# Two feed-forward stages around a state-space layer: layer 1 multiplied once per batch for z and for its twist

## The reference

```python
gf = _global_net(z.mean(axis=1), ...)                 # one number for a batch
out = z
for _ in range(3):                                    # NUM_CYCLES
    h = gelu(out @ w1 + b1); h = gelu(h @ w2 + b2); h = gelu(h @ w3 + b3)
    tf = sigmoid(h @ w4 + b4)                         # one number for a token
    coupling = 0.1 + adaptive_range * (0.7 * gf + 0.3 * tf - 0.5) * 2.0
    out = out + coupling * twist(out)                 # [o_r,o_i,p_r,p_i] -> [p_r,-p_i,-o_r,o_i]
```

## Time and profile before

| | |
|---|---|
| median of 3 runs | 1359.43 us (1358.84 to 1360.23) |
| the profiled execution | 1361.13 us, its span from first to last instruction 1359.1 us |
| TensorE matmul busy | 1133.3 us, 83% of the span |
| VectorE busy | 1149.4 us, 85% |
| ScalarE busy | 737.0 us, 54% |
| GpSimd busy | 871.9 us, 64% |
| mean granted TensorE clock | 0.949 of full speed |

### The profile page before, as it was taken

The page is one execution under the profiler, slowest core; times in us unless marked ns, Lnnn a source line. Parts: engine busy times, 40 slices in busy tenths (PEclk is TensorE's granted clock), DMA queues, the critical chain, the costliest instruction groups (busy, mean ns, idle before and its releaser), DMA issues. The chain is left out here.

```text
span 1359.1 us, 10889 instructions
## 1 busy us (share of the span) xinstructions
PE 1133.3 (83%) x2880; PEld 491.7 (36%) x2880; DVE 1149.4 (85%) x1628; ACT 737.0 (54%) x1267; POOL 871.9 (64%) x390
## 2 busy tenths in 40 slices
PE   3999985769778889878978987987896978799997
PEld 2344432223333334324324333433432423434443
DVE  4656676399999999999999999999999999746556
ACT  2554444757655756755656674665674433355442
POOL 0000000699989999998999999899999998000000
PEclk9999996798999999999999989999998988999998
DMA  6000000444535444354453544435435442000001
GB/s 201 0 1 1 0 0 1 140 135 146 180 102 185 132 149 155 124 185 134 146 179 113 174 146 139 151 124 186 154 127 184 155 156 78 0 0 0 32 31 62
DMA packets 46940, 146.47 MB, mean 108 GB/s; under 512 B 4448, under 2 KB 13280, under 8 KB 46880
## 3 DMA queue, kind: packets, MB, share of 16 engines
q1 hardware_dynamic: 46384, 144.96, 31.8%
q10 hardware_dynamic: 496, 0.82, 0.2%
HBM read 141.05 MB, written 4.72 MB: 107 GB/s over the span
## 5 line engine op out<-in xcount | busy, mean ns | idle before, releaser
L905 POOL TENSOR_TENSOR m_u<-m_dx,m_brow 128x1024 f32<-128x1024 f32 x256 | 596.7, 2355 | 1.0 <-DVE m_a_bank L988 0.9
L791 ACT ACTIVATE m_a_bank<-m_delta,m_negA 128x512 f32<-128x512 f32 x512 | 335.0, 683 | 171.6 <-DVE m_hc L1000 131.3
L1134 PE MATMUL m_y_bank<-m_hc,ident 128*128 128x512 f32 x640 | 333.1, 646 | 103.7 <-DVE m_hc L1000 103.7
L917 POOL TENSOR_TENSOR m_hc_pool<-m_hid,m_crow 128x1024 f32<-128x1024 f32 x96 | 226.0, 2354 | 28.5 <-DVE m_hid L988 28.1
L1134 PEld LDWEIGHTS m_y_bank<-m_hc,ident 128*128 128x128 f32 x640 | 120.1, 201 | 290.7 <-DVE m_hc L1000 170.5
L1000 DVE TENSOR_TENSOR m_hc<-m_a_bank,m_crow 128x512 f32<-128x512 f32 x320 | 202.5, 673 | 0.0
L926 POOL TENSOR_TENSOR m_dx<-m_delta,m_x 128x1024 f32<-128x1024 f32 x16 | 37.7, 2357 | 249.5 <-ACT m_delta L863 249.5
L988 DVE TENSOR_TENSOR_SCAN m_a_bank<-m_a_bank,m_carry,m_u 128x512 f32<-128x512 f32 x160 | 196.1, 1270 | 1.1 <-ACT m_a_bank L791 0.8
L988 DVE TENSOR_TENSOR_SCAN m_a_bank<-m_a_bank,m_u 128x512 f32<-128x512 f32 x160 | 186.6, 1212 | 7.1 <-POOL m_u L905 3.5
L1134 PE MATMUL m_y_bank<-m_hc_pool,ident 128*128 128x512 f32 x384 | 184.4, 603 | 5.6 <-POOL m_hc_pool L917 5.6
L333 PE MATMUL f_bank<-f_state,w 128*128 128x512 f32 x384 | 181.9, 603 | 0.0
(11 more groups left out here) (111 smaller groups left out, 1168.8 us busy)
## 6 DMA issues: line engine op xcount, KB each, us to landing
m_brow<-bc_rows SPq DMA_DIRECT2D x128, 512.0 KB, 4.8
m_crow<-bc_rows SPq DMA_DIRECT2D x128, 512.0 KB, 3.9
x_tok<-x_in SPq DMA_DIRECT2D x4, 1024.0 KB, 8.6
out<-x_tok SPq DMA_DIRECT2D x3, 1024.0 KB, 4.4
w<-w_in SPq DMA_DIRECT2D x1, 1024.0 KB, 11.4
out<-x_tok SPq DMA_DIRECT2D x2, 512.0 KB, 3.0
w<-w_in SPq DMA_DIRECT2D x1, 750.0 KB, 10.4
w<-w_in ACTq DMA_DIRECT2D x1, 512.0 KB, 5.9
```

The source lines that it names most:

```text
L791: nc.scalar.activation(a_bank[K % 2][:, j, :], delta[:, i % 2, c, :], ACT.Exp, scale=negA[:, c, n:n + 1]).then_inc(S["a"], 1)
L905: nc.gpsimd.tensor_tensor(u[:, K % U_RING, :, :], dx[:, i % 2, 2 * q:2 * q + 2, :], brow[:, K // 2 % ROW_RING, K % 2, :].unsqueeze(1).to_b ...
L917: nc.gpsimd.tensor_tensor(hc_pool[:, before % POOL_RING, :, :], hid[:, before % POOL_RING, :, :], crow[:, K // 2 % ROW_RING, K % 2, :].uns ...
L1134: op = nc.tensor.matmul(y_bank[:, j, :], ident[:, :], source[:, before % ring, j, :], start=False, stop=K % PASS == PASS - 1)
```

## The change

Only `ffn` changes, and the order of the channels in the inputs: the host permutes the quarters of the channels so that `twist` of the two channel halves `[z0, z1]` is `[z1, -z0]`.

- TensorE multiplies `A = z @ w1` and `B = twist(z) @ w1` once for each batch and half (kinds `A` and `B`, L440 and L441, four multiplications each, `B` with a negated copy `neg_w` of half the weights). ScalarE copies both from PSUM into SBUF (`a` and `b_`, 1024 elements in one instruction, L570). `layer1` is gone from the steps.
- `gelu1` (L508) reads SBUF: `a` in cycle 0, `a1` in cycle 1, `a` again in cycle 2.
- VectorE makes these. `update` (L242, L255, L257) runs in cycles 0 and 1 only: the coupling, written over the tanh, then one product and one sum of 1024 elements, with the coupling row repeated for both output halves. After cycle 0, `turn` (L265, L270) brings `b_` to the next state's twist with four instructions of 1024.
- `z_tok` holds all 32 tiles. The last state isn't formed with channels on partitions. SyncE copies one row of each coupling of cycles 0 and 1 into `stack` by DMA, the last tanh goes there too, TensorE transposes `stack` (kind `C`, L448), VectorE works out the coefficients of each token (`coefficients`, 15 instructions of 8 elements), and `finish` applies them in token order: ScalarE `x * scale + bias` (L548, 8 instructions of 256), then VectorE two sums of 128 channels for each tile (L322, L324). For batch 2 (`ALONE`) VectorE does ScalarE's part too (L314).
- The table is now `BESIDE`: (step and place on TensorE, kind, batch, half or layer, step and place on ScalarE). The output is stored in four whole batches.

The core of the diff:

```diff
+    BESIDE = [
...
+        (5, 0, "g", 3, 0, 5, 1), (5, 1, "g", 3, 1, 5, 2), (5, 1, "B", 3, 0, 5, 2), (5, 2, "g", 3, 2, 5, 3),
+        (6, 0, "C", 0, 0, None, None), (6, 1, "B", 3, 1, 6, 2), (7, 0, "C", 1, 0, None, None),
...
+            def normalise(b):
+                for t in range(BT):
+                    o = b * BT + t
+                    nc.vector.tensor_scalar(z_tok[:, o, :], x_tok[:, o, :], moments[:, o, 0:1], rstd[:, o:o + 1],
+                                            ALU.subtract, ALU.mult).then_inc(z_ready, 1)
...
+                b, n = batch(s), coupled(s, h)
+                c = cpl[:, b % 2, half(h)]
+                dve.wait_ge(th_ready, s * HALVES + h + 1)
+                nc.vector.tensor_scalar(c, c, slope[:, 0:1], base[:, b:b + 1], ALU.mult, ALU.add).then_inc(coupling, 1)
+                dve.wait_ge(coupling, n)
...
+                nc.vector.tensor_tensor(to, b_[:, b % AB_RING, :, half(h)], over_m(c), ALU.mult).then_inc(scaled, 1)
+                dve.wait_ge(scaled, n)
+                nc.vector.tensor_tensor(to, to, other, ALU.add).then_inc(a_ready, 1)
+            def turn(s):
...
+                for h in range(HALVES):
+                    nc.vector.tensor_tensor(part[:, h], a[:, b % AB_RING, :, half(h)],
+                                            over_m(cpl[:, b % 2, half(h)]), ALU.mult).then_inc(part_ready, 1)
+                for h in range(HALVES):
+                    from_b = b_[:, b % AB_RING, :, half(h)]
+                    dve.wait_ge(part_ready, turned(s, h))
+                    nc.vector.tensor_tensor(from_b, from_b, part[:, h], ALU.subtract).then_inc(b_ready, 1)
...
+            def coefficients(b):
...
+                dve.wait_ge(beside_done, done_count(("C", b, 0)))
+                if b > 0:
+                    wait_added(dve, b - 1)
...
+                for j in range(2):
+                    nc.vector.tensor_copy(at(j), src[:, :, 32 + j])
+                nc.vector.tensor_scalar(at(2), src[:, :, 0], slope[:, 0:1], base[:, b:b + 1],
+                                        ALU.mult, ALU.add).then_inc(coef_read, 1)
+                dve.wait_ge(coef_read, b + 1)
...
+            def finish(b):
+                coefficients(b)
+                if b == ALONE:
+                    for t in range(BT):
+                        at = b * BT + t
+                        op = nc.vector.scalar_tensor_tensor(x_tok[:, at, :], z_tok[:, at, :], coef[:, 7, t:t + 1],
+                                                            x_tok[:, at, :], ALU.mult, ALU.add)
+                    op.then_inc(first_added, 1)
+                    dve.wait_ge(first_added, 1)
+                for t in range(BT):
+                    at, c = b * BT + t, slice(t, t + 1)
+                    if b != ALONE:
+                        dve.wait_ge(first_act, (b - (b > ALONE)) * BT + t + 1)
+                    nc.vector.scalar_tensor_tensor(x_tok[:, at, :P], z_tok[:, at, P:], coef[:, 8, c], x_tok[:, at, :P],
+                                                   ALU.mult, ALU.add).then_inc(added, 1)
+                    nc.vector.scalar_tensor_tensor(x_tok[:, at, P:], z_tok[:, at, :P], coef[:, 9, c], x_tok[:, at, P:],
+                                                   ALU.mult, ALU.add).then_inc(added, 1)
...
+            for s in range(1, STEPS + 1):
+                if cycle(s - 1) < CYCLES - 1:
                     for h in range(HALVES):
                         update(s - 1, h)
                 if s == 1:
                     coupling_base(1)
+                if cycle(s - 1) == 0:
+                    turn(s - 1)
+                if s == 1:
+                    normalise(3)
+                if s in (3, 4):
+                    sum_up(s - 1)
+                if s in (5, 6):
+                    coupling_base(s - 3)
+                if s in (6, 7):
+                    finish(s - 6)
                 if s in (9, 10) and measure_next:
                     measure(s - 9)
+            finish(2)
+            if measure_next:
+                measure(2)
+            finish(3)
...
+                elif kind in ("A", "B"):
+                    wait_read(pe, ("T", b, n))
+                    if kind == "B":
+                        pe.wait_ge(constants, 1)
+                    for m in range(KD):
+                        ms = slice(m * P, (m + 1) * P)
+                        if kind == "A":
+                            first, second = w(w256, W256, "w1", 0)[:, ms], w(w256, W256, "w1", 1)[:, ms]
+                        else:
+                            first, second = neg_w[:, ms], w(w256, W256, "w1", 0)[:, ms]
+                        nc.tensor.matmul(out[:, m, :], first, z[:, b % 2, 0, half(n)], start=True, stop=False)
+                        last = nc.tensor.matmul(out[:, m, :], second, z[:, b % 2, 1, half(n)], start=False, stop=True)
+                elif kind == "C":
+                    s = step(b, CYCLES - 1)
+                    pe.wait_ge(th_ready, (s + 1) * HALVES)
+                    for h in range(HALVES):
+                        wait_kept(pe, step(b, CYCLES - 2), h)
+                    for t in range(BT):
+                        last = nc.tensor.transpose(out[:, 0, t * STACK:(t + 1) * STACK],
+                                                   stack[:, b % 2, t * P:(t + 1) * P], ident[0:STACK, 0:STACK])
...
+                b, o = batch(s), W128["b1"][0] + m
+                if cycle(s) == 0:
+                    wait_read(act, ("A", b, h))
+                    source = a[:, b % AB_RING, m, half(h)]
+                else:
+                    act.wait_ge(a_ready, coupled(step(b, cycle(s) - 1), h))
+                    source = (a1[:, b % 2] if cycle(s) == 1 else a[:, b % AB_RING])[:, m, half(h)]
+                if s > 0:
+                    act.wait_ge(l2_done, (s - 1) * HALVES + h + 1)
+                nc.scalar.activation(h1[:, m, half(h)], source, ACT.Gelu, bias=w128[:, o:o + 1]).then_inc(h1_ready, 1)
...
+            def finish(b):
+                act.wait_ge(coef_ready, 2 * b + 2)
+                for t in range(BT):
+                    at = b * BT + t
+                    nc.scalar.activation(x_tok[:, at, :], x_tok[:, at, :], ACT.Identity, scale=coef[:, 10, t:t + 1],
+                                         bias=coef[:, 11, t:t + 1]).then_inc(first_act, 1)
...
+                if s in (6, 7):
+                    finish(s - 6)
...
+            finish(3)
...
+            for s in range(STEPS):
+                if cycle(s) < CYCLES - 1:
+                    for h in range(HALVES):
+                        b, row = batch(s), 32 + cycle(s)
+                        sp.wait_ge(coupling, coupled(s, h))
+                        if b >= 2:
+                            sp.wait_ge(beside_done, done_count(("C", b - 2, 0)))
+                        sp.dma_start(stack[row:row + 1, b % 2, half(h)], cpl[0:1, b % 2, half(h)])\
+                            .then_inc(kept[b % 2][h], 16)```

Three places where the order of an engine changes. The names: `f_a`, `f_b`, `f_z` are SBUF, `f_pair` and `f_bank` PSUM, `f_h` is `h1`, `h2` or `h3`.

TensorE at the end of step 4 and the beginning of step 5, before:

```order
L345 MATMUL f1_bank5<-f1_h1,w256 128x512 [waits f1_h2r,f1_h1r]
L345 MATMUL f1_bank5<-f1_h1,w256 128x512
L333 MATMUL f1_bank0<-f1_state,w256 128x512 [waits f1_updated,f1_h1r]
L333 MATMUL f1_bank0<-f1_state,w256 128x512
L355 MATMUL f1_bank6<-f1_h2,w128 64x512 [waits f1_thr,f1_h2r]
```

More of the change, by code:

```diff
@@ L148, in done_count, with wait_kept, half, over_m @@
         def done_count(use):
[L150 removed]
+            return USES.index(use) + 1
         def wait_read(engine, use):
[L154 to L163 removed]
+            before = USES[:USES.index(use) + 1]
+            of_c = sum(u[0] == "C" for u in before)
+            if use[0] == "C":
+                engine.wait_ge(coef_read, of_c)
+            else:
+                engine.wait_ge(beside_read, len(before) - of_c)
+        def wait_kept(engine, s, h):
+            engine.wait_ge(kept[batch(s) % 2][h], 16 * (batch(s) // 2 * (CYCLES - 1) + cycle(s) + 1))
+        def half(h):
+            return slice(h * BANK, (h + 1) * BANK)
+        def over_m(t):
+            return t.unsqueeze(1).to_broadcast([P, KD, BANK])
+        def wait_added(engine, b):
+            engine.wait_ge(added, (b + 1) * BT * 2)
         @block.vector
@@ L405, in _, with beside @@
+                last.then_inc(beside_done, 1)
+            def beside(s, place):
+                for at in BESIDE:
+                    if at[:2] == (s, place):
+                        work(at[2:5])
             if load_sem is not None:
                 pe.wait_ge(load_sem["ident"], 2)
-            side(HEAD, 0)
-            if load_sem is not None:
                 pe.wait_ge(load_sem["weights"], 48)
+            beside(HEAD, 0)
             for s in range(STEPS):
-                layer1(s, 0, 0)
+                beside(s, 0)
@@ L492, in _ @@
             for s in range(STEPS):
+                read(s, 0)
```

(14 more changed lines are left out.)

415 lines of the change are left out of this document (186 added, 229 removed), and 9 rows, old and new, of the table BESIDE.

## The result

| | before | after |
|---|---|---|
| median | 1359.72 us (4 runs) | 1406.84 us (1405.54 to 1407.84, 4 runs) |
| the profiled execution | 1361.13 us, span 1359.1 | 1407.68 us, span 1405.8 |
| TensorE matmul busy | 1133.3 us | 1080.9 us |
| VectorE busy | 1149.4 us | 1165.5 us |
| ScalarE busy | 737.0 us | 784.4 us |

A forecast was written before the change was run, and what follows sets the result against it. TensorE was taken to bound a stage. Head, steps 0 to 5, steps 5 to 11 and tail gave 12.6 us (stage 2) and 12.9 (stage 1), with the clock's 16 41.5: 1361.13 becomes 1402.6, median 1401, range 1376 to 1428.

The forecast's parts named there:

- head, to layer 3 of step 0: Start of each stage: layer 3 of step 0 starts at 1200.1 instead of 1190.2, +10.0 us a stage.
- steps 0 to 5: Layer 3 of step 0 to step 5: TensorE work 70.6 us plus waits 11.3, against 71.3 before, +10.6 a stage.
- steps 5 to 11: Last six steps: the loop through ScalarE and VectorE decides; 70.3 us, before 80.8, so -10.5 a stage.
- tail: End of a stage, VectorE finishing batch 2 alone, then batch 3: +2.5 us in stage 2, +1.9 in stage 1.
- TensorE's step 1 stands behind ScalarE's wait: Head: ScalarE's wait for the moments of batches 2 and 3 holds up all of TensorE's step 1.
- wait of 7.2 us: Start of step 5: global net layer 1 of batch 3 waits for VectorE's sum, behind the update of step 3.
- L548's wait of 11.1 us: After step 7, ScalarE idles 11.1 us in finish(1) for coefficients behind VectorE's update and turn.
- The clock: TensorE drops to half speed after pauses: 8 us a stage, between 0 and 20; +16 in all.
- Rival (a): TensorE's clock stays up, since no pause but two is long: 1385 us, chance 0.16.
- Unit prices: Assumed times of single operations on TensorE, VectorE and ScalarE, such as 1.25 us for 1024 elements on VectorE.
- Rival (c): A VectorE instruction of 1024 costs no more than one of 512, 0.69 for 1.25: 1353.5 us, chance 0.06.
- rival (b): TensorE's clock stays at 1.2 GHz from step 5 on, 20 us a stage: 1425 us, chance 0.14.

The follow-up runs named there:

- e4_fillers: Changed kernel plus TensorE multiplications whose result nobody reads, placed in its pauses, order unchanged: 1390.01 us against 1406.84.
- e6_head: Changed kernel with only ScalarE's order at the start of a stage changed, root for batch 1 ahead of its copy of A: 1403.57 us against 1406.84.
- e2_g3_late: Changed kernel with the three global net layers of batch 3 one to two places later on TensorE and ScalarE: 1390.32 us against 1406.84.
- e1_coef_early: Changed kernel with VectorE working out batch 1's coefficients ahead of the update of step 6: 1390.38 us against 1406.84.
- e5_half_products: Changed kernel with VectorE's products, sums and turns on 512 elements instead of 1024, not the whole computation: 1368.95 us against 1406.84.

## Why the prediction was right, step by step

The forecast of 1401 (1376 to 1428, slower) was right in sign and, but for the cause of the head, in mechanism, and 6 us short. By its own terms, for each stage, on its axis (the first table load of stage 2 is at 1188.29 instead of 1167.84, so 20.45 is taken off):

| term | predicted | stage 1 | stage 2 |
|---|---|---|---|
| head, to layer 3 of step 0 | +10.0 | +7.2 | +9.8 |
| steps 0 to 5 | +10.6 | +10.0 | +10.0 |
| clock in steps 0 to 5 | +3 | +6.5 | +6.6 |
| steps 5 to 11 | -10.5 | -7.3 | -9.0 |
| clock in steps 5 to 11 | +5 | +2.3 | +4.2 |
| tail | +1.9, +2.5 | +3.9 | +4.7 |

The rows without clock are those of e4_fillers; its last steps in stage 1 still have some clock in them, so the split there is a bound. The two stages sum up to 22.6 and 26.3, the state-space layer took 2.2 less in this execution (it varies between 950.9 and 953.4 over all kernels), and 46.7 is the difference of the spans. These 2.2 are no merit of the forecast: by the stages alone it was 7.4 short.

- **Head.** Layer 3 of step 0 came at 1199.96 on the axis, forecast 1200.1. In stage 1 the head is 2.6 us shorter; that the loading of the inputs covers some of it is likely, but I hadn't looked at it and no run tests it. The sentence that TensorE's step 1 stands behind ScalarE's wait named the wrong releaser: e6_head takes that wait away and gains 0.8 us. The right number came from a walk in which TensorE's own eight blocks end at nearly the same time; as far as the cause goes, that was luck.
- **Steps 0 to 5.** The wait of 7.2 us was 7.12, ended by the instruction named, and 70.6 + 11.3 = 81.9 was 81.31 at full clock. e2_g3_late shows it to be on the path.
- **Steps 5 to 11.** L548's wait of 11.1 us was 10.69, TensorE's pause of 15 was 14.87; 70.3 us at full clock were 71.75. e1_coef_early and e5_half_products show that it is VectorE and the order that decide, and not TensorE.
- **The clock** was the first term mis-sized, 8 a stage for 9 to 11. For steps 0 to 5 I took 3; it was 6.5. Two things were missing there: a pause of 2.09 us at the start of step 4, for the sum of batch 2, was in my walk with 1.7, and I priced no clock behind it, though the row with a pause of 2.23 before a stretch at 0.59 said so; and behind the pause of 7.1 us layer 3 and half of B ran at half clock (1.97, 2.07, 1.91). The upper end of 20 a stage was far off, since not every wait lowered the clock: behind those of 1.47 us in steps 9 and 11 a block took 1.98 (in e1_coef_early, behind one of 1.47 us in step 11, it took 3.66). Rival (a), no clock cost, would have been near with the fillers in: 1385 against 1390.01.
- **The tail** was the second, +4.7 and +3.9 for +2.5 and +1.9. The 16 sums of 128 channels are 0.26 apart and not 0.2 (4.2 for 3.2), eight of 256 take 3.26 and not 2.7, and the store of 1 MB lands in 4.8 instead of 4.4. The signal that each of the 16 gives isn't what takes the time: L314's eight instructions of 256 signal once together, and at 0.40 apart they need the same 0.13 beyond 1.05 ns an element as those of 128.
- **Unit prices** held elsewhere: 1.23 for 1024 elements (1.25 taken), 2.99 for half an update (3.1), 4.54 for a turn (4.7), 2.05 for the coefficients (2.1), 4.04 for ScalarE's eight (4.1). Cheaper than taken were ScalarE's copy of 1024 (1.02 for 1.15) and the transposes C (0.68 for 1.2). Rival (c) fell with the 1.23: against 0.69 for 512, the second 512 elements add 0.54 us, 1.05 ns each. (The Trainium skill, VectorE: DVE Perf Modes, has the one fp32 element a cycle for a product in the section Mode 2×_2P — use both read ports for one tensor; the section that the prediction names gives only the reason. The trace agrees as far as it goes: it has no product of 1024 at a higher rate than one of 512.) And rival (b) fell with the clock of 1.00 in 1354 to 1366.
